# A four-layer graph network on one core: layer 2's nodes and layer 3's tables in one stage, and longer loops over the edge blocks

## The reference

```python
# layer 2
deg = max(count of edges by dst, 1);  r = rsqrt(deg)
diff = [r[src], r[dst]][:, None, :] - mu                      # E x 4 x 2
gw = exp(sum(-0.5 * diff * diff / (1e-15 + sigma * sigma)))   # E x 4
xt = (x @ g).reshape(n, 4, 64)
agg = sum over k of segment_sum(gw[:, k, None] * xt[src, k], dst)
x = layernorm(x + x + relu(agg / deg + x @ root + bias))
# layer 3
h = relu(concat(x[src], x[dst], edge_attr) @ W1.T + b1)
agg = segment_sum(h @ W2.T + b2, dst)
gi, gh = agg @ w_ih.T + b_ih, x @ w_hh.T + b_hh
r, z = sigmoid(i_r + h_r), sigmoid(i_z + h_z);  c = tanh(i_n + r * h_n)
x = layernorm(x + (1 - z) * c + z * x)
```

## Time and profile before

| what | us |
|---|---|
| median of 3 runs | 8629.86 (8614.71 to 8640.16) |
| the profiled execution, its own time | 8661.29 |
| span of the profiled execution | 8658.9 |
| TensorE matmul busy | 5190.3 (60%) |
| TensorE weight load busy | 4348.2 (50%) |
| VectorE busy | 4583.7 (53%) |
| ScalarE busy | 1567.8 (18%) |
| GpSimd busy | 4332.5 (50%) |

### The profile page before, as it was taken

The page is one execution under the profiler, slowest core; times in us unless marked ns, Lnnn a source line. Parts: engine busy times, 40 slices in busy tenths (PEclk is TensorE's granted clock), DMA queues, the critical chain, the costliest instruction groups (busy, mean ns, idle before and its releaser), DMA issues. The chain is left out here.

```text
span 8658.9 us, 136636 instructions
## 1 busy us (share of the span) xinstructions
PE 5190.3 (60%) x47914; PEld 4348.2 (50%) x47915; DVE 4583.7 (53%) x8920; ACT 1567.8 (18%) x3149; POOL 4332.5 (50%) x4149
## 2 busy tenths in 40 slices
PE   2555555555555323253565448888886677777776
PEld 1334333433334222243554338888885566666665
DVE  4555555555555434353454554444445566666665
ACT  1111111111111100011111320000002333333332
POOL 3666666666666455513555613333330555555562
PEclk7776777667677666656766659999995789889897
DMA  3222222222222445521000301111111333333332
GB/s 110 88 86 82 82 87 87 87 84 87 87 87 73 84 91 100 98 24 55 22 21 21 119 16 21 21 21 21 21 20 19 121 97 96 93 97 100 95 95 52
DMA packets 379331, 599.64 MB, mean 69 GB/s; under 512 B 148462, under 2 KB 308192, under 8 KB 363811
## 3 DMA queue, kind: packets, MB, share of 16 engines
q1 hardware_dynamic: 235177, 472.07, 17.6%
q0 software_dynamic: 133216, 116.93, 6.6%
q10 hardware_dynamic: 10454, 4.04, 0.2%
HBM read 517.27 MB, written 213.23 MB: 84 GB/s over the span
## 5 line engine op out<-in xcount | busy, mean ns | idle before, releaser
L340 POOL DMA_INDIRECT pay_d<-row,place x1632 | 1728.3, 1059 | 1140.1 <-issue 531.1
L1954 PE MATMUL g_win<-g_hot,y_part 128*128 128x128 bf16 x14994 | 971.7, 227 | 263.5 <-issue 161.4
L443 PE MATMUL win<-onehot,val 128*128 128x128 f32 x4998 | 846.3, 336 | 409.5 <-ACT onehot L356 206.2
L1954 PEld LDWEIGHTS g_win<-g_hot,y_part 128*128 128x128 bf16 x14994 | 908.6, 102 | 319.2 <-issue 212.1
L443 PEld LDWEIGHTS win<-onehot,val 128*128 128x128 f32 x4998 | 768.1, 241 | 598.8 <-ACT onehot L356 349.9
L1934 POOL DMA_INDIRECT g_x<-xg_d,g_row x459 | 509.4, 1110 | 937.2 <-PE g_win L1954 723.1
L2407 POOL DMA_INDIRECT m_from_src<-from_src_d,m_row x459 | 507.1, 1105 | 633.4 <-PE m_pre L2443 402.6
L546 DVE TENSOR_TENSOR hot<-near_dve,drel 128x896 bf16<-128x896 bf16 x357 | 222.6, 624 | 1070.4 <-remote 772.7
L781 POOL DMA_INDIRECT r_x<-in_x,r_row x459 | 436.6, 951 | 448.4 <-PEq L821 254.3
L1278 POOL DMA_INDIRECT sorted_d<-s_row,s_place x459 | 444.6, 969 | 414.7 <-DVE s_place L1394 232.9
L2410 POOL DMA_INDIRECT m_from_dst<-from_dst_d,m_row x459 | 564.4, 1230 | 139.9 <-issue 135.9
(11 more groups left out here) (452 smaller groups left out, 10694.8 us busy)
## 6 DMA issues: line engine op xcount, KB each, us to landing
m_hot_t<-drow_d SPq DMA_DIRECT2D x52, 1568.0 KB
scan_d<-in_none SPq DMA_DIRECT2D x51, 1034.2 KB
lo_row<-lo_d SPq DMA_DIRECT2D x51, 1024.0 KB
m_grid<-pay_d SPq DMA_DIRECT2D x52, 882.0 KB
pay_d<-in_fill SPq DMA_DIRECT2D x51, 882.0 KB
grid<-pay_d SPq DMA_DIRECT2D x51, 882.0 KB
pay_d<-in_fill SPq DMA_DIRECT2D x51, 648.0 KB
row<-in_pay SPq DMA_DIRECT2D x51, 576.0 KB
```

Of the source, the lines that this page charges most:

```text
L340: pool.indirect_dma_start(a["pay_d"][:, :], bass.IndirectOffsetOnAxis(ap=place[j][:, c:c + 1], axis=0), row[j][:, c, :], None).then_inc(ro ...
L443: last = mm(win[:, :], val[u % 2][:, s, :], onehot[u % 2][:, s, :], start=(u == 0 and s == 0), stop=(u == NS - 1 and s == SUB - 1))
L1954: last = mm(win[:, h, 0:W], k.y[q][:, t, h * P:(h + 1) * P], hot[u][:, s, :], start=(t == 0 and q == 0), stop=(t == NT - 1 and q == 2))
```

## The change

Five edits.

1. `over_rounds` takes the number of thirds per turn. Layers 2 and 3 use 8, that is two turns of 24 blocks and three blocks outside; layers 0 and 1 keep 2.
2. Layer 2's tables also transpose x and multiply it with root (and the bias, by a row of ones), into `k.p`. The accumulators are zeroed by GpSimd. The destination's gain is multiplied by 1/degree once.
3. Layer 2's nodes and layer 3's tables become one stage, written out by block: while VectorE finishes block b of layer 2, TensorE prepares block b+1's products with g, transposes b-1 and multiplies b-2, and the splitting for b-3 runs. The products with g use 128 x 128 weights with zeroed quarters and read the accumulators in place.
4. In layer 3's edges, the comparison at a block's end serves the next block; the one at u=1 goes.
5. In layer 2's edges, the grid's comparison reads 0..127 in fp32 in place of bf16.

```diff
-def over_rounds(eng, z, k, body):
+def over_rounds(eng, z, k, body, turn=2):
...
-        with eng.Fori(0, thirds // 2) as i:
-            for h in range(2):
+        with eng.Fori(0, thirds // turn) as i:
+            for h in range(turn):
...
@@ layer2_tables @@
             def _(pool):
+                for b in range(2):
+                    pool.memset(xt[b][D:D + 1, :], 1.0).then_inc(ones_set, 1)
+                    pool.drain()
                 pool.tensor_copy(xg[:, :, 0:D], ...).then_inc(xg_ready, 1)
+                pool.memset(k.acc0[:, :], 0.0)
+                pool.memset(k.acc1[:, 2 * TB * P:z.NC], 0.0)
+                pool.wait_ge(own_ready, z.NB)
+                pool.memset(k.acc1[:, 0:2 * TB * P], 0.0)
...
                 for b in range(z.NB):
+                    if b + 1 < z.NB:
+                        keep_turned(b + 1)
                     act.wait_ge(scaled_ready, 4 * (b + 1))
                     keep(b, 0)
+                    keep_own(b)
...
-                v.memset(k.acc0[:, :], 0.0)
-                v.memset(k.acc1[:, :], 0.0)
@@ layer2_edges, and so for every engine there and in layer3_edges @@
-                over_rounds(sp, z, k, body)
+                over_rounds(sp, z, k, body, turn=8)
...
-                        v.tensor_tensor(hot[u][:, :, :].rearrange("p s (w q) -> p s w q", q=2), by_twos(k.iota_b[:, :], SUB),
-                                        two_each(twos(drel[j][:, u * SUB:(u + 1) * SUB]), W), ALU.is_equal).then_inc(hot_ready, 1)
+                        v.tensor_tensor(hot[u][:, :, :], k.iota[:, :].unsqueeze(1).to_broadcast([P, SUB, W]),
+                                        twos(drel[j][:, u * SUB:(u + 1) * SUB])[:, :, 0:1].to_broadcast([P, SUB, W]),
+                                        ALU.is_equal).then_inc(hot_ready, 1)
@@ layer2_nodes: the old loop and layer3_tables go; the new stage @@
+                for b in range(1, NB + 2):              # TensorE, after mix(0), mix(1) and the weights
+                    if b <= NB:
+                        turn_nodes(b - 1)
+                    if 0 <= b - 2:
+                        multiply(b - 2)
+                    if b + 1 < NB:
+                        mix(b + 1)
...
+                for b in range(NB + 3):                 # ScalarE, after twice(0)
+                    if 0 <= b - 3:
+                        middle(b - 3)
+                    if 1 <= b <= NB:
+                        keep_turned(b - 1)
+                    if b < NB:
+                        square(b)
+                        root(b)
+                    if b + 1 < NB:
+                        twice(b + 1)
...
+                    if 0 <= b - 2 < NB:
+                        keep_products(b - 2)
+                        high(b - 2)
...
+                def combine(b):
+                    x = nodes_of(b)
+                    for h, (t0, t1_) in enumerate(halves):
+                        dve.wait_ge(conv_ready, 2 * b + h + 1)
+                        v.tensor_tensor(prod[:, t0:t1_, :]..., conv_ps[h]..., k.gain[...].to_broadcast(...),
+                                        ALU.mult).then_inc(conv_read, 1)
+                    dve.drain()
+                    v.tensor_tensor(half_sum[:, :, :], prod[:, :, 0:2 * D], prod[:, :, 2 * D:4 * D], ALU.add)
+                    dve.drain()
+                    v.tensor_tensor(conv[:, :, :], half_sum[:, :, 0:D], half_sum[:, :, D:2 * D], ALU.add)
+                    dve.drain()
+                    v.tensor_tensor(conv[:, :, :], conv[:, :, :], k.p[:, tiles_of(b), :], ALU.add)
+                    dve.drain()
+                    dve.wait_ge(double_ready, b + 1)
+                    v.scalar_tensor_tensor(out=x, in0=conv[:, :, :], scalar=0.0, in1=double[b % 2][:, :, :], op0=ALU.max, op1=ALU.add)
...
+                for b in range(NB + 3):                 # VectorE
+                    if 0 <= b - 3:
+                        take_high(b - 3)
+                    if b < NB:
+                        combine(b)
+                    if b == 0:
+                        dve.wait_ge(w_mixed, 2)
+                        dve.wait_ge(w_in, 16 * 9)
+                        v.tensor_tensor(k.wx[:, 0:3 * D], k.wx[:, 0:3 * D], w_ps[1], ALU.add).then_inc(wx_kept, 1)
+                    if 0 <= b - 3:
+                        take_middle(b - 3)
+                    if b < NB:
+                        spread(b)
+                        scale(b)
@@ layer3_edges @@
+                def relative(n, m, j):
+                    dve.wait_ge(row_in[j], m * 16 + 16)
+                    v.tensor_copy(dst_f[:, :], row[j][:, :, AT_DST].bitcast(i32))
+                    dve.drain()
+                    v.tensor_scalar(rel_next[:, :], dst_f[:, :], k.group[:, at(n)], None, ALU.subtract)
+
+                def second(n, nxt, nm, nj):
+                    v.tensor_copy(rel[:, 0, :], rel_next[:, :])
                     v.tensor_scalar(cols[:, :], k.shift[:, :], k.group[0:1, at(n)], float(z.NP), ALU.add, ALU.min)
                     dve.drain()
-                    v.tensor_scalar(rel[:, :], dst_f[:, :], k.group[:, at(n)], None, ALU.subtract)
-                    dve.drain()
-                    expand()
+                    relative(nxt, nm, nj)
...
-                        v.tensor_scalar(rel[:, :], rel[:, :], -float(WS), None, ALU.add)
+                        v.tensor_scalar(rel[:, bass.ds(w + 1, 1), :], rel[:, bass.ds(w, 1), :], -float(WS), None, ALU.add)
+                        dve.drain()
+                        v.tensor_copy(rel[:, bass.ds(count, 1), :], rel_next[:, :].unsqueeze(1))
...
-                        expand()
+                        expand(rel[:, bass.ds(w + 1, 1), :])
```

519 lines of the change are left out of this document (285 added, 234 removed).

## The result

The changed kernel took 8254.4 us (median of 4 runs, 8238.5 to 8260.5), the kernel before 8635.0 in the same measurement: ratio 0.956, 95% interval 0.953 to 0.958.

What follows compares the result with a forecast made beforehand. Both edge stages were taken as set by TensorE and what feeds it; in layer 2's nodes engines take turns. Terms -30 - 42 - 3 - 0 - 4 - 90 = -169 us, giving 8461 us against the median 8629.9; range 8385 to 8540.

Steps and rivals of the forecast that it cites:

- fp32 compare in layer 2's edges: Layer 2's edges: each fp32 compare takes 0.47 us more on VectorE, covered by TensorE's sums; price 0, uncovered 24 us.
- rival 2: Layer 2's edges: fp32 compares lengthen GpSimd's gathers and TensorE's short halts may grow 1 us, +51, to 8512 us; chance 0.15.
- The prediction's own sign of being wrong: Wrong if ordinary blocks of either edge stage change by over 1 us, or the merged stage takes over 135.
- the loops in layer 2: Layer 2's edges: longer turns remove six of seven loop returns at 5.0 us each, -30 us; bounds 24 to 36.
- In layer 3 the term: Layer 3's edges: longer turns remove six of seven loop returns at 7 us each, -42 us; bounds 24 to 60.
- Rival 3: Both edge stages: the loops' gain is absent because the longer body pays the refilling elsewhere, 8533 us; chance 0.08.
- The reused comparison: Layer 3's edges: one comparison per block less on VectorE, mostly off the path; 0.05 us a block, -3 us.
- Rival 1: Layer 3's edges: the freed comparison counts, blocks 1 us or so faster, 50 to 80 us less, about 8395; chance 0.13.
- Layer 2's tables: Layer 2's tables: memsets leaving VectorE save 9.5 us, ScalarE's turned-x copies add 5.7; net -4, bounds -10 to +8.
- The merged stage: Layer 2's nodes with layer 3's tables: 195 us becomes 105, a gain of 90; bounds 60 to 100.
- the upper bound: Merged layer 2 nodes and layer 3 tables: 100 us gain if TensorE's clock rises.
- Rival 4: Both edge stages: longer bodies make engines load code, slower; decides from 1.7 us a block, 8715 us at 2.5; chance 0.04.

## Why the prediction was wrong, step by step

**What failed.** "*fp32 compare in layer 2's edges.* ... Price 0." It priced the comparison's own 0.47 us on VectorE and found it covered, which held: VectorE's busy time rose by 162 us and the stage did not wait for it. What it left out is what the comparison does to its neighbour GpSimd, and so to TensorE. The term measured -181 to -194 us, most of the 225 us by which the stage missed its forecast. The prediction had seen the halts ("which nothing explains") and the stretched gather (2.10 for 0.94 us), and joined them with the wrong sign, in rival 2: gathers that stretch should make the halts grow. They stretched, from 1110 to 1255 ns as that rival said, and the halts were gone: stretching spaced the gathers out, and pacing them by waits removes the halts as well. The prediction's own sign of being wrong, ordinary blocks that change by over 1 us, came in layer 2: 26.5 to 21.9.

**Mis-sized: the loops in layer 2.** -30 forecast, -61 to -73 measured. The size was read as the excess of a return over its neighbours; those neighbours held 4.7 us of halts each themselves. Against blocks without halts, a return costs 9 to 12 us at this pace and 7 at the other in loops of six blocks; the single one that is left costs 3.8 and 7.3 us in the two executions of the changed kernel. In layer 3 the term was right to a few us: -42 forecast, -33 at the slower and -39 at the faster pace. Rival 3, no gain from loops, is ruled out by the run with the loops alone (0.988, 0.987 to 0.990).

**The reused comparison.** -3 forecast, -22 at this pace, that is 0.43 us a block, and -59, or 1.16 a block, at the faster one, where less of anything else stands in the way. The 0.19 us of the earlier trace rows was the wait at one mark of one block. Rival 1 was right in kind and, at this pace, about a third of its lower end.

**Layer 2's tables.** -4 forecast, +3.2 measured, inside the bounds given (-10 to +8). Of the 9.5 us for the memsets taken off VectorE, 8.3 were lost because GpSimd's memsets shut VectorE's next steps out. With the memsets behind the gains the stage takes 86.8 us, 5.1 less than before: near the forecast. VectorE's period in the block loop grew by 0.86 us (9.63 to 10.49), where 0.95 was worked out.

**The merged stage.** 105 us forecast, 99.4 measured; -95 for -90. VectorE multiplies by the reciprocal root at these times, one row a block:
```profile
6278.21 0.62 DVE L2390 TENSOR_TENSOR x_nodes<-x_nodes,l_std 128x448 f32<-128x448 f32 x1
...
6287.57 0.62 DVE L2390 TENSOR_TENSOR x_nodes<-x_nodes,l_std 128x448 f32<-128x448 f32 x1
...
6296.93 0.62 DVE L2390 TENSOR_TENSOR x_nodes<-x_nodes,l_std 128x448 f32<-128x448 f32 x1
```
The early blocks take 9.4 us where 9.5 was worked out; the later ones 11.2, 11.2, 13.2 and 11.2 for 11.7; the tail from the last x to the next stage 16.7 for 17.2. The start is what was too long: the weights' mixing was done 14.4 us into the stage for 19.9, and the first x at 17 for 22. TensorE ran some of its products at 2.4 GHz (mean granted clock 0.71, before 0.50), the case that the upper bound names.

**Rival 4**, longer code costing time, has nothing for it: 296 pieces on q8 for 322, and the ordinary blocks of neither stage got longer.

What stays open is why TensorE slows down when gathers come close. That it does so only at the slower pace (dense gathers at the faster one left ordinary blocks at 21.6 us) says that it takes something besides. TensorE waits for no semaphore and no engine that the profile names. What makes the pace is open too. It isn't the chip, as two chips showed both. It isn't in every stage: the placing stage took 2820 to 2905 us at the slower pace and 2271 to 2282 at the faster, layer 0's nodes 102.0 at both. Nor do the gathers' packets in layer 2's edges differ: 118 ns as a mean in the kernel before, 116 and 121 in two runs of the faster pace. Also open is what the changed kernel gains at the faster pace; it was not run there itself, only with its comparison in other forms (0.965 to 0.967 without further edits) and with late memsets and longer loops in layers 0 and 1 (0.965).

## What to carry to other kernels

Halts that nothing explains are a term of the sum, with a sign that can go either way: before pricing an edit at nothing because it is covered, ask what it does to the timing of the engines beside it. A cost read as "this block minus its neighbours" is only as good as the neighbours. And when an engine is given work to free another, look whether the two can run at once; a wait of one line decided whether the memsets were free.

## What the hardware did that was not expected

At the slower pace three gathers of GpSimd that started within 2.8 us slowed TensorE to one to six multiplications per 0.7 us, which added 3 to 9 us to a block; with three in 2.84 us or more it ran on. The same kernel ran 8.6 or 7.0 ms in different measurements, and only at the first pace did this occur.

Of the clock: in one block of the kernel before TensorE halted from 5410.7 to 5414.7 and the granted clock fell to half at 5415.35, for 3.4 us, so after the halts and not ahead of them. The mean granted over halting blocks was 0.87 to 0.96 of 2.4 GHz, beside 1.00 in paced ones of the same trace.

A bf16 comparison of 896 elements takes 623 ns in pairs and 1086 ns with a value broadcast at step zero. A VectorE step of eight elements took 5.32 us beside a memset of GpSimd.
